# Second edge convolution of a graph network: the one-hot of the eighth tile as a compare of two tensors, and the cast to high parts as a product with ones

## What is computed

```python
w = _edge_weights(edge_attr, fc0_w1, fc0_b1, fc0_w2, fc0_b2)   # a small network per edge
...
out = _seg_mean(msg, src, N)                                    # first edge convolution
...
w = _edge_weights(edge_attr, fc1_w1, fc1_b1, fc1_w2, fc1_b2)
wa = w[:, :NS * NS].reshape(E, NS, NS)
wb = w[:, NS * NS:].reshape(E, NV, NS)
s = s0[dst]
v = v0[dst]
path_a = jnp.einsum('ei,eij->ej', s, wa)
path_b = jnp.einsum('eic,ec,eij->ej', v, sh1, wb) * float(1.0 / np.sqrt(3.0))
msg = (path_a + path_b) * float(1.0 / np.sqrt(NS + NV))
node1 = _seg_mean(msg, src, N)                                  # second edge convolution
```

## Time and profile before

| what | value |
|---|---|
| median of 3 runs | 4025.93 us (4010.98 to 4033.75) |
| the profiled execution: its time, its span | 4011.01 us, 4009.2 us |
| busy share of the span: PE, DVE, ACT, POOL | 86%, 82%, 72%, 70% |
| second edge convolution in the trace | about 1,398 to 2,400 us |
| mean granted TensorE clock | 0.937 of full |

### The profile page before, as it was taken

The page is one execution under the profiler, slowest core; times in us unless marked ns, Lnnn a source line. Parts: engine busy times, 40 slices in busy tenths (PEclk is TensorE's granted clock), DMA queues, the critical chain, the costliest instruction groups (busy, mean ns, idle before and its releaser), DMA issues.

```text
span 4009.2 us, 105599 instructions
## 1 busy us (share of the span) xinstructions
PE 3432.0 (86%) x28555; PEld 2877.3 (72%) x28556; DVE 3285.0 (82%) x6355; ACT 2881.7 (72%) x3881; POOL 2810.9 (70%) x2751
## 2 busy tenths in 40 slices
PE   3459999999999699999999995778886888878887
PEld 3438888888888577777777775678885777757775
DVE  7789999999999788888888886678876887767876
ACT  2139999999999599999999994455533566646665
POOL 4447777777777477777777766777764777657774
PEclk9979999999999899999999997788777999989999
DMA  6011111111111321111111111111111222222221
GB/s 81 27 14 24 26 24 24 24 24 24 26 24 24 22 31 29 31 31 29 31 29 31 31 27 23 30 27 30 30 24 27 44 44 42 37 36 44 43 41 30
DMA packets 285656, 124.23 MB, mean 31 GB/s; under 512 B 179726, under 2 KB 260338, under 8 KB 285622
## 3 DMA queue, kind: packets, MB, share of 16 engines
q1 hardware_dynamic: 186838, 87.92, 9.5%
q0 software_dynamic: 84672, 29.47, 8.6%
q10 hardware_dynamic: 14112, 6.43, 0.7%
HBM read 121.80 MB, written 1.78 MB: 31 GB/s over the span
## 4 chain that ended last, share of the span: by engine, by line
PE 35%; POOL 24%; issue 22%; DVE 10%; DMA 4%; DVEq 4%; POOLq 0%; SPq 0%; ACT 0%; ACTq 0%
POOL gb L457 17%; PE ps L762 10%; PE ps L778 10%; POOL gb L447 7%; PE ps L883 6%; PE ps L768 2%; PE ps L899 2%; PE ps L832 2%; DMA eat<-vtab 2%; DMA gb<-table,idx 2%; PE ps L676 1%; DVE rest L1030 1%; DVE oht L1417 1%; DVE xt L1150 1%; PE ps L895 1%
## 5 line engine op out<-in xcount | busy, mean ns | idle before, releaser
L457 POOL DMA_INDIRECT gb<-table,idx x1568 | 1620.0, 1033 | 567.4 <-issue 450.9
L447 POOL DMA_INDIRECT gb<-table,idx x1078 | 1100.3, 1021 | 491.2 <-issue 448.9
L762 PE MATMUL ps<-big,oh 128*128 128x290 f32 (+1 forms) x7840 | 1265.9, 308 | 1.7 <-DVE big L1190 1.7
L762 PEld LDWEIGHTS ps<-big,oh 128*128 128x128 f32 x7840 | 1071.4, 191 | 125.2 <-DVE big L1190 2.2
L778 PE MATMUL ps<-w,ht 128*128 128x320 f32 x3136 | 1011.6, 446 | 119.9 <-DVE xt L1150 107.5
L557 ACT ACTIVATE oh<-iota_f,src_n 128x640 fp32r<-128x640 f32 x1372 | 1024.7, 816 | 0.0
L560 ACT ACTIVATE oh<-oh,ones 128x2560 fp32r<-128x2560 f32 (+1 forms) x392 | 849.6, 2167 | 12.8
L778 PEld LDWEIGHTS ps<-w,ht 128*128 128x128 f32 x3136 | 558.1, 191 | 382.3 <-DVE xt L1150 177.8
L1150 DVE TENSOR_TENSOR xt<-ps,gb 128x640 f32<-128x640 f32 x784 | 643.2, 821 | 80.1 <-PE ps L778 28.7
L642 ACT ACTIVATE rest<-rest,dst_f x1220 | 383.0, 389 | 319.0 <-PE ps L899 276.2
L1158 DVE TENSOR_REDUCE msg<-xt 128x80 f32<-128x1280 f32 (+1 forms) x392 | 580.5, 1481 | 0.0
(11 more groups left out here) (226 smaller groups left out, 2856.0 us busy)
## 6 DMA issues: line engine op xcount, KB each, us to landing
gb<-table,idx POOLq DMA_INDIRECT x2646, 2.3
eat<-in_eat SPq DMA_DIRECT2D x196, 192.0 KB, 2.4
eat<-vtab SPq DMA_DIRECT2D x98, 160.0 KB
eat<-vtab SPq DMA_DIRECT2D x49, 256.0 KB
eat<-vtab SPq DMA_DIRECT2D x98, 128.0 KB
rest<-in_edge_attr ACTq DMA_DIRECT2D x98, 64.0 KB, 1.8
idx<-in_src SPq DMA_DIRECT2D x245, 4.0 KB
idx<-in_dst SPq DMA_DIRECT2D x196, 4.0 KB, 1.6
```

The lines of the kernel that those rows point to most:

```text
L447: nc.gpsimd.indirect_dma_start(out=(gb if p == 2 else gr)[:, b, t, 0:tabw[p]], out_offset=None, in_=tabs[p], in_offset=bass.IndirectOffset ...
L457: nc.gpsimd.indirect_dma_start(out=gb[:, b, t, 0:tabw[p]], out_offset=None, in_=tabs[p], in_offset=bass.IndirectOffsetOnAxis(ap=idx[:, b, ...
L762: mm = nc.tensor.matmul(out, oh5[:, b, t, c * P:(c + 1) * P], big[:, b, t, 0:W], start=False, stop=False, skip_group_check=True)
```

## The change

In the second edge convolution only, VectorE's one-hot of tile 7 becomes a TENSOR_TENSOR whose second input is the one column of `src_v`, repeated 640 times, where it was a TENSOR_SCALAR with that column as scalar; and the high part of `msg` is written by a TENSOR_TENSOR product with ones, where it was a copy with a cast. Per super that is one instruction of 128 x 640 and two of 128 x 64. The number, the order, the waits and the semaphores of the instructions are the same on every engine. In the changed file the lines behind the edit lie lower: the product with ones stands at L1180, `low_half` at L1185, `spread_half` at L1194, `vprod` at L1213, and the compare at L1235.

```diff
--- before.py
+++ after.py
@@ -1173,8 +1173,12 @@
...
-                    V.tensor_copy(parts[l][:, b, 4 * h:4 * h + 4, 0:W],
-                                  msg[:, b, 4 * h:4 * h + 4, m0:m0 + W]).then_inc(m_hi[l], 1)
+                    high, rows = parts[l][:, b, 4 * h:4 * h + 4, 0:W], msg[:, b, 4 * h:4 * h + 4, m0:m0 + W]
+                    if l == 0:
+                        V.tensor_copy(high, rows).then_inc(m_hi[l], 1)
+                    else:
+                        V.tensor_tensor(high, rows, ones[:, 0:4 * W].rearrange("p (t f) -> p t f", t=4),
+                                        ALU.mult).then_inc(m_hi[l], 1)
...
@@ -1224,8 +1228,12 @@
...
-                    V.tensor_scalar(oh5[:, b, AT, :], iota_f[:, 0:CW], src_v[:, bass.ds(s, 1), AT], None,
-                                    ALU.is_equal).then_inc(l_done[l], 1)
+                    if l == 0:
+                        V.tensor_scalar(oh5[:, b, AT, :], iota_f[:, 0:CW], src_v[:, bass.ds(s, 1), AT], None,
+                                        ALU.is_equal).then_inc(l_done[l], 1)
+                    else:
+                        V.tensor_tensor(oh5[:, b, AT, :], iota_f[:, 0:CW], src_v[:, bass.ds(s, 1), AT].broadcast_to([P, CW]),
+                                        ALU.is_equal).then_inc(l_done[l], 1)
```

## The result

The changed kernel takes 4053.14 us (median of 4 runs, 4045.01 to 4060.88) against 4018.45 (4 runs) before: ratio 1.0083, 95% interval 1.0059 to 1.0106. It is slower by about 33 us by the ratio (35 by the medians), where 29 were forecast.

A forecast was written before the change was run, and what follows sets the result against it. GpSimd's gathers were taken to bound the stage; the compare holds one gather 0.30 us longer in 96 supers, 29 us. Added to the 4025.9 us median this gave 4055 us, range 4037 to 4072, or 4021 to 4072 including Rival A.

The forecast's parts named there:

- Gathers pace the stage: Second edge convolution: GpSimd's eight gathers set the super's 10.42 us, 10.02 undisturbed plus 0.40 in longer gathers.
- the hold: A gather needing something 0.12 us after its start waits while VectorE runs an instruction with two SBUF inputs or the TENSOR_SCALAR.
- What the compare costs VectorE: VectorE, per super: compare 0.82 us against 0.55, products 0.21 against 0.18; 0.34 more, covered by its 1.28 wait for gathers.
- The price on GpSimd: Fourth gather of each super, under the compare: held 0.35 us instead of 0.05, 0.30 more, 29 us over 96 supers.
- The second collision: A later gather of each super, held 0.36 us by the spread, stays held because both move with the compare's end.
- A repeated column counts as an SBUF input: Compare's column repeated 640 times holds gathers fully, taken from edge-network L1014, where a gather lasted 0.74 us more.
- The base: Whole kernel: the 29 us were added to 4025.9 us, the median of three runs, giving 4055 us.
- Rival A: Compare leaves gathers alone, its repeated column being fetched once, and the phase stays: -5 us, 4021; chance 0.10.
- Rival B: Compare holds no gather and VectorE's shift also undoes the spread's collision: -29 us, 3997; chance 0.04.
- ScalarE's floor: Second edge convolution: ScalarE is busy some 10.05 to 10.12 us a super, limiting a gain to 0.30 a super.
- C: TensorE's added idle time costs it full clock, so it bounds the stage: +200 us; chance 0.02.
- D: VectorE becomes the bound because gathers hold it in turn: +35 us or more; chance 0.04.

The follow-up runs named there:

- experiment 4: Kernel before, with the second edge convolution's small one-hot `oh_h` in PSUM, so the spread has one SBUF input: 3976.21 us against 4016.9, ratio 0.9903.
- experiment 6: Changed kernel with the cast put back and both the compare's repeated column and `oh_h` in PSUM: 3972.61 us against 4020.11 before, ratio 0.9884.
- experiment 3: Changed kernel with the cast put back and the compare's repeated column read from PSUM: 4004.51 us against 4016.9 before, ratio 0.9968.
- experiment 1: Changed kernel with the cast put back, so the compare alone is changed: 4041.71 us against 4016.9 before, ratio 1.0064.
- experiment 9: Changed kernel with its compare cut into two instructions of 320 columns: 3986.67 us against 4020.3 before, ratio 0.9916.
- experiment 10: Changed kernel with `oh_h` in PSUM, run again to profile another execution: 3984.94 us against 4020.3 before, ratio 0.9914.
- experiment 5: Changed kernel with the small one-hot `oh_h` of the second edge convolution in PSUM: 3987.44 us against 4020.11 before, ratio 0.9921.

## Why the prediction was right, point by point

- *Gathers pace the stage.* Shown: taking the hold away (experiments 4 and 6) took 0.42 us from each super though VectorE's work was the same or more.
- *How it was read.* One reading under it was wrong. L1209 at 2015.85 does not wait for the gather that began at 2014.47, since none lands in under 2.2 us. The eighth of its super is the one at 2013.22, 2.63 us earlier. The distances that the sum uses are taken from the rows and don't depend on it.

```profile
DMA to landing us min/median/max: 2.2/2.3/2.5
```

- *What the compare costs VectorE.* 816 ns against 0.82, and 212 ns for the product with ones against 0.21. VectorE's wait of 1.27 us a super stayed, so this was covered; experiments 3 and 6 have nearly the same length and are faster.
- *The price on GpSimd.* The gather under the compare begins 3.70 us after L1213 (1968.15 - 1964.45), where 3.72 was forecast, and 10.72 us a super was forecast and measured; gather mean 1036 forecast, 1035 measured; stage +28.0 against 29. The mechanism is shown by experiment 3, where only the place of one operand differs from experiment 1: -13 us against +26.
- *The second collision stays.* Shown by the 1.31 at 1971.00, under a spread that begins 2.04 us after the compare's end, as forecast. Experiments 3 and 9 show that it was worth asking: there the spread shifts against the gathers, and the sign of the result turns.
- *A repeated column counts as an SBUF input.* Taken from L1014; experiments 1 and 3, which differ in where the column lies, confirm it.
- *The base.* That 4055 lies within 2 us of 4053.14 is luck: two errors cancel. The median of before is 4018.45 now, 7 lower than what was shown, and the medians are 35 apart instead of 29. In the two profiled executions the stage gives 28.0 of it, and the rest lies outside the stage.
- *Rival A* fell with the 1.29 gather. The probe that the Trainium skill's page "SBUF — State Buffer" reports, a GpSimd transfer that `tensor_tensor` did not stall, does not carry over to these indirect gathers. The section's rule on two SBUF inputs agrees with them, if what a gather needs is a read of SBUF; experiment 3, where the compare writes the same SBUF tile and holds nothing, fits that. *Rival B's* arithmetic was sound: made true by experiment 3, it gave both outcomes. One number of it was off: ScalarE's floor, the super's length when it never waits, is 10.00 us (experiments 4 and 6), not 10.05 to 10.12. *C* is out (clock 1.00). *D* is out (wait unchanged).
- The gain in experiment 4 was 41 us where 26 to 33 were expected: the term that was mis-sized is ScalarE's floor, and L1227's own 0.05 went too, since no gather lasts over 964 ns there.
- *The TENSOR_SCALAR.* That it holds gathers as well is a reading of the earlier trace rows, and the 0.10 there fits it to 0.02 us; the gather at 2599.22 in experiment 10 is held from under another one. No experiment isolates it, and what about this instruction holds them stays open.

## What to carry to other kernels

Where GpSimd's indirect gathers pace a stage, look for gathers longer than the median and at what VectorE runs 0.12 us after their start: an operand in PSUM, or a long instruction cut in two, can be worth more than VectorE's own time. The cut helped here in part by its phase, so it may not elsewhere. An edit that makes VectorE a little longer or shorter also shifts its later instructions against the gathers, so its price can have either sign; work out the phase before counting nanoseconds. Read the stage's period from the trace, since the total also carries the other stages, here the 34 us by which the edge network's holds differed between two executions of one kernel.

## What was not expected of the hardware

- The hold does not begin with the record, if a gather's reading point lies 0.12 us after its start. In experiment 3 a spread that began with the gather at 1653.04 let it through and was itself 0.04 us longer; one that began 0.02 us before it held it 0.67 us. In that stage of experiment 3 the border is sharp: no gather that began up to 0.3 us ahead of a spread, or with it, was held, and every one that began 7 ns to 0.57 us behind it was, to the spread's end. So it goes to whoever is first. The 0.12 us, for the gather's reading point as for the hold's begin, rests on the hold ending with VectorE's record. What the traces give by themselves are the border and the 1.12 us from that end to the next gather.
- Between two such instructions, back to back, there can be room for a waiting gather: it came through between the halves in experiment 9 and between two L1014 in the earlier trace rows. But it is not always so: the gather of 3.92 us in experiment 10 waited through both L1014. What decides is open.
- One program can settle in either of two phases of the same stage, 10.01 or 10.37 us a super (experiments 5 and 10, one profiled execution each), for all of the stretch from 1600 to 2350 us.
